# A two-layer cross-attention and feed-forward kernel in fp32: four places in its order are rearranged, and TensorE's buffers start on multiples of 256 bytes

## What is computed

```
x = x + mlstm(layernorm(x), ctx, ctx)      # 16 heads of 32, gates, decay matrix, head norm
x = x + moe(layernorm(x))                  # rms norm, router, best 2 of 8 experts (512->256->512), shared expert
x = x + attention(layernorm(x), ctx)       # q, k, v = 512 -> 2048, rms norm of q and k, 16 heads of 128,
                                           # two softmaxes: context tokens before 257 and from 257 on
x = x + last_ffn(layernorm(x))             # ternary weight (round(w/mean|w|), clipped) * mean|w|, plus bias
...
mlstm:  C = (q k^T / sqrt(32)) * D;  h = (C / max(|sum C|, exp(-max log D))) v;  head norm of h
moe:    sum over the two chosen experts of p_e * down_e(silu(gate_e(t)) * up_e(t)), plus the shared expert
q = rms_norm(x @ q_w + q_b);  k = rms_norm(ctx @ k_w + k_b);  v = ctx @ v_w + v_b;  out = softmax(q k^T / sqrt(128)) v @ o_w + o_b
```

## Time and profile before

| what | us |
|---|---|
| median of 3 runs (lowest, highest) | 1330.21 (1328.85, 1332.80) |
| the profiled execution, its own time | 1327.5 |
| its span, first to last instruction | 1325.8 |
| PE busy | 1272.9 (96%) |
| DVE busy | 840.4 (63%) |
| ACT busy | 739.3 (56%) |
| POOL busy | 391.7 (30%) |
| mean granted TensorE clock | 0.993 of full |

### The profile page before, as it was taken

How to read it: one execution, slowest core, us unless ns; L and a number is a source line. 1 busy time by engine, 2 the same in 40 slices (tenths; PEclk the granted TensorE clock), 3 DMA queues, 4 the chain that set the end, 5 groups by cost and what they waited for, 6 DMA issues and landing times. The chain is left out here.

```text
span 1325.8 us, 24459 instructions
## 1 busy us (share of the span) xinstructions
PE 1272.9 (96%) x7380; PEld 1056.3 (80%) x7381; DVE 840.4 (63%) x1611; ACT 739.3 (56%) x1829; POOL 391.7 (30%) x363
## 2 busy tenths in 40 slices
PE   7999997998999899999999999999999999999998
PEld 6787875776777778788877778878888888888987
DVE  3644647778679863544445577463587777777965
ACT  5225538788886441445555455554786556556551
POOL 0111015273728016599531332163010000000041
PEclk9999999999999899999999999999999999999999
DMA  7897399887865394665669776555375565555403
GB/s 251 306 365 257 133 319 347 264 274 249 280 213 183 68 359 171 221 189 174 205 206 317 238 267 191 180 192 192 119 231 162 157 165 158 158 170 153 120 26 127
DMA packets 165831, 277.06 MB, mean 209 GB/s; under 512 B 29744, under 2 KB 57136, under 8 KB 165488
## 3 DMA queue, kind: packets, MB, share of 16 engines
q1 hardware_dynamic: 139648, 219.46, 51.8%
q0 software_dynamic: 8960, 30.41, 7.0%
q10 hardware_dynamic: 17136, 26.09, 5.3%
HBM read 167.11 MB, written 108.80 MB: 208 GB/s over the span
## 5 line engine op out<-in xcount | busy, mean ns | idle before, releaser
L121 PE MATMUL banks<-of_shared_split,key_lead 128*128 128x512 f32 x256 | 104.6, 409 | 6.7 <-DVE key_trail L1427 6.3
L3019 ACT ACTIVATE prob<-banks,attend_row,rq 128x128 f32<-128x128 f32 x248 | 110.5, 470 | 0.0
L3032 ACT ACTIVATE attend_ol<-banks,of_attend_vbias 128x512 fp32r<-128x512 f32 x64 | 44.2, 691 | 116.5 <-PE banks L3231 116.5
L121 PE MATMUL banks<-wo,attend_ol 128*128 (+1 forms) x256 | 106.2, 415 | 0.0
L121 PE MATMUL banks<-queries_rows_split,queries_wl 128*128 128x512 f32 x256 | 100.9, 394 | 0.2 <-DVE queries_rows_split L2655 0.2
L123 PE MATMUL banks<-wo,attend_ot 128*128 (+1 forms) x256 | 100.7, 393 | 0.0
L123 PE MATMUL banks<-of_shared_split,key_trail 128*128 128x512 f32 x256 | 100.6, 393 | 0.0
L122 PE MATMUL banks<-of_shared_split,key_lead 128*128 128x512 f32 x256 | 100.1, 391 | 0.0
L122 PE MATMUL banks<-wo,attend_ol 128*128 (+1 forms) x256 | 99.9, 390 | 0.0
L123 PE MATMUL banks<-queries_rows_split,queries_wt 128*128 128x512 f32 x256 | 99.8, 390 | 0.0
L122 PE MATMUL banks<-queries_rows_split,queries_wl 128*128 128x512 f32 x256 | 99.8, 390 | 0.0
(11 more groups left out here) (407 smaller groups left out, 3507.3 us busy)
## 6 DMA issues: line engine op xcount, KB each, us to landing
mlstm_gmax<-running_max SPq DMA_DIRECT2D x32, 512.0 KB, 6.4
k_heads<-heads_key ACTq DMA_DIRECT2D x64, 256.0 KB, 4.9
q_heads<-queries_head SPq DMA_DIRECT2D x64, 256.0 KB, 2.8
q_ahead<-q_heads SPq DMA_DIRECT2D x64, 256.0 KB, 4.1
of_attend_k<-k_heads SPq DMA_DIRECT2D x60, 256.0 KB, 4.0
of_attend_v<-v_heads SPq DMA_DIRECT2D x60, 256.0 KB, 3.3
key_raw<-in_L_xattn_ki_w SPq DMA_DIRECT2D x20, 512.0 KB, 5.8
sorted_rows<-of_shared_split SPq DMA_DIRECT2D x2, 5120.0 KB, 27.3
```

The source lines that it names most:

```text
L121: nc.tensor.matmul(out, lead_l, lead_r, start=first, stop=False)
L3019: ins = nc.scalar.activation(prob[:, j % 2, b, :], ps[:, j % 2, b * S:(b + 1) * S], ACT.Exp, bias=row[:, j % 2, 1, b:b + 1], scale=rq[:, b ...
L3032: nc.scalar.activation(ol[:, par, j, :], ps[:, 4 + j % 2, :], ACT.Identity, bias=vbias[:, bass.ds(quad_of(it) * 4 + j, 1)]).then_inc(ol_do ...
```

## The change

It has seven parts.

1. Start: POOL's fills move from their own block into that of `values_and_gates`. SP loads the first context group in four pieces of 128 columns, each ahead of a weight load. PE begins with 10 idle transposes and turns 0 and 1; turn c+2 stands behind unit chunk c, and turns 4 to 7 behind chunk 2. ACT's `keep_even` stands one step later.
2. Values: DVE's trail cuts of weight quad 1 stand one unit later.
3. Heads, opening: a key unit more stands ahead of step 4's scores and the later ones move up; DVE does two `context_sum` before the first `decayed`, and decayed(2) and (3) earlier; SP issues `next_raw(0, 1)` before the body.
4. Heads, end: the 16 token sums stand behind the last four key units, three each, and the last four ahead of the third tail unit. DVE's `finish(PER)` stands ahead of the head scaling; ACT's `keep_tail(2)` stands behind the root.
5. Second pass: the down weights of experts 6 and 7 are cut by POOL after its first two parked loads, which no longer wait for tiles; ACT cuts and keeps tile 4 between the first copies of results.
6. Queries' end: 20 idle transposes for 14.
7. Places: padding tensors and new constants put of_shared_split, the context, keys, routed tiles, queries, `parked`, `wo` and the attention's tiles on multiples of 256 bytes.

```diff
-PARKED = 146144
+PARKED = 146432
 TAIL = (1, G - 1)
-TAIL_W, TAIL_V = 119328, 193568
-WO, Q_AHEAD = 129760, 195296
+TAIL_W, TAIL_V = 119552, 193792
+WO, Q_AHEAD = 130048, 195584
 PROB = Q_AHEAD + 4 * N * 4
-X_LEAD, X_TRAIL = 115232, 59712
-KEY_RAW, KEY_SPLIT = 160288, 195104
+X_LEAD, X_TRAIL = 115456, 59712
+KEY_RAW, KEY_SPLIT = 160512, 195328
...
-        TRAILS = {OPENS[q + 1] - (6 if q < QUADS - 2 else 5) + c: (q + 1, c) for q in range(QUADS - 1) for c in range(C)}
+        TRAILS = {OPENS[q + 1] - (6 if 0 < q < QUADS - 2 else 5) + c: (q + 1, c) for q in range(QUADS - 1) for c in range(C)}
...
-            load_ctx(0)
             for c in range(C):
+                sp.dma_start(stage[0][:, :, c * P:(c + 1) * P],
+                             a["ctx_2048"][0:GB, :, c * P:(c + 1) * P].rearrange("b s d -> s b d")).then_inc(ctx_first[c], 16)
                 sp.dma_start(raw[:, c, :], w_dram[c * P:(c + 1) * P, 0:N]).then_inc(first_loaded[c], 16)
...
+            setup(nc, K, pool, blank, made)
...
+            keep_even(0)
             turn_plain(C)
+            keep_even(2)
             turn_plain(C + 1)
-            keep_even(0)
-            keep_even(2)
...
-            for t in range(C):
-                turn(t)
+            pe.wait_ge(made, 1)
+            keep_busy(nc, ps[:, 0, :], K.ident, 10)
+            turn(0)
+            turn(1)
             for c in range(C):
                 first_chunk(c)
-                if c < C - 1:
-                    turn(C + c)
+                if c + 2 < C:
+                    turn(c + 2)
                 if c == C - 2:
-                    turn(C + c + 1)
+                    for t in range(C, 2 * C):
+                        turn(t)
...
-    OPENING = (0, 1, 2, 3, 5, 6, 8, 9, 11, 12, 14, 15)
+    OPENING = (-1, 0, 1, 2, 3, 5, 6, 8, 9, 11, 13, 15)
...
+            next_raw(0, 1)
...
-            for b in range(TAIL_IN_HEADS):
+            for b in range(TAIL_IN_HEADS - 1):
                 keep_tail(b)
             act.wait_ge(sums, 1)
             nc.scalar.activation(rk[:], ps[:, 2, 0:B], ACT.Sqrt, scale=1.0 / INNER, bias=K.eps6[:, 0:1]).then_inc(rk_done, 1)
             act.wait_ge(late_agg, 1)
             nc.scalar.activation(K.rstd[:, EARLY:], K.mv[:, EARLY:, 1], ACT.Sqrt, bias=K.eps5[:, 0:1]).then_inc(late_root, 1)
+            keep_tail(TAIL_IN_HEADS - 1)
...
-                    if n + 1 < PER or g + 1 < G:
+                    if (n + 1 < PER or g + 1 < G) and not (first and n < 3):
                         decayed(g, n + 1, first)
+                    if first and n == 0:
+                        decayed(g, 2, first)
                     if first:
                         keys_at(g, n, 1, weight_trail, first)
+                    if first and n == 1:
+                        decayed(g, 3, first)
...
-            for b in range(GB):
-                context_sum(0, b)
+            context_sum(0, 0)
+            context_sum(0, 1)
             decayed(0, 0, True)
+            context_sum(0, 2)
+            context_sum(0, 3)
+            decayed(0, 1, True)
...
+            finish(PER)
             dve.wait_ge(fac_done, G)
             for b in range(GB):
                 r = slice(b * H0, (b + 1) * H0)
                 ins = nc.vector.tensor_tensor(sq[:, r, :], raw_heads(last)[:, r, :],
                                               small[:, 5, r].unsqueeze(2).broadcast_to([P, H0, DH0]), ALU.mult)
             own(ins)
-            finish(PER)
...
+            def token_sums(tokens):
+                for b in tokens:
+                    ins = nc.tensor.matmul(ps[:, 2, b:b + 1], total[:, b * S:(b + 1) * S], K.ones[:, 0:1],
+                                           start=True, stop=True)
+                return ins
+
+            pe.wait_ge(total_done, CLOSES[G - 2] + 1)
+            pe.wait_ge(c_done, UNITS)
             for m in range(PER - LAG, PER):
                 keys(G - 1, m)
+                token_sums(range(3 * (m - PER + LAG), 3 * (m - PER + LAG) + 3))
             pe.wait_ge(tail_loaded, 32)
             pe.wait_ge(h_done, G * QUADS)
             tail_unit(nc, ps, split, tail_w, 0).then_inc(tail_product, 1)
             for b in range(1, TAIL_IN_HEADS):
                 if TAIL_BANKS[b] in KEY_BANKS:
                     pe.wait_ge(ksq_done, UNITS)
+                if b == TAIL_IN_HEADS - 1:
+                    pe.wait_ge(total_done, UNITS)
+                    token_sums(range((G - 1) * GB, B)).then_inc(sums, 1)
                 tail_unit(nc, ps, split, tail_w, b).then_inc(tail_product, 1)
-            pe.wait_ge(total_done, UNITS)
-            for b in range(B):
-                ins = nc.tensor.matmul(ps[:, 2, b:b + 1], total[:, b * S:(b + 1) * S], K.ones[:, 0:1],
-                                       start=True, stop=True)
-            ins.then_inc(sums, 1)
...
+    outer.sb("line", [P, 40])
...
+    inner.sb("line", [P, 16])
...
+            BY_POOL = (E - 2, E - 1)
...
-                pool.wait_ge(down, 1 + 5 * piece // 2)
+                if piece == 2:
+                    for e in BY_POOL:
+                        pool.wait_ge(dn_loaded[e % 4], 32)
+                        pool.wait_ge(dn_ready, e)
+                        n, ins = cut_by_pool(wd[:, e], raw_dn[e % 4], n)
+                        ins.then_inc(dn_ready, 1)
+                if piece >= 2:
+                    pool.wait_ge(down, 1 + 5 * piece // 2)
...
-            for e in range(4, E):
+            for e in range(4, E - 2):
                 act.wait_ge(dn_loaded[e % 4], 32)
                 nc.scalar.activation(wd[:, e, 0], raw_dn[e % 4], ACT.Copy).then_inc(dn_lead, 1)
-            for n in range(2):
+            keep((0, 0))
+            hidden_lead((0, H_DEEP))
+            for n in range(1, H_DEEP - 1):
                 keep((0, n))
-            second(act, second_slot, skip=H_DEEP)
+            second(act, second_slot, skip=H_DEEP + 1)
...
-            keep_busy(nc, ps[:, 7, :], K.ident, 14)
+            keep_busy(nc, ps[:, 7, :], K.ident, 20)
...
+    ph.sb("line", [P, 16])
...
+        kept("attend_line", [P, 56])
```

36 lines of the change are left out of this document (18 added, 18 removed).

## The result

The changed kernel took 1336.98 us (median of 11 runs, 1334.16 to 1340.91), the kernel before 1330.78 (11 runs, 1327.82 to 1336.16). The ratio is 1.0043, with a 95% interval of 1.0028 to 1.0059. I had forecast 1321 and a range up to 1332, so both the sign and the range were wrong. The profiled execution took 1339.07 us, its span is 1337.4.

What follows compares the result with a forecast made beforehand. PE was taken to bound the kernel, busy 1272.9 of 1325.8 us. The terms -2.0 - 2.3 - 2.0 + 0.6 + 2.3 - 0.8 - 4.5 sum to -8.7 us, so 1321 on the median, range 1303 to 1332.

Steps and rivals of the forecast that it cites:

- Heads, opening: Opening of the heads: an earlier key unit and DVE's earlier `cmat` shorten PE's waits; -2.0 us, bounds 0 and -4.2.
- the slower rival: All operands: equal offsets at 0 are the worst pair, +23 us on the pace, about 1349; chance 0.06.
- Second pass: Routed second pass: tile 4's wait goes, but tile 8 waits 5.0 us for POOL; +2.3 us, bounds -3.9 and +6.
- goes as meant: Second pass: tile 8 does not wait for POOL, so -3.9 replaces +2.3, 1315 us; chance 0.09.
- Places: Value, key, shared, x and tail products: multiples of 256 bytes bring 226.7 ns; -4.5 us, bounds 0 and -9.
- the floor at 226.7 ns: Matmul pace: 226.7 ns, the best that any window showed at any offset, taken as the floor.
- the fast one: All 4,250 matmuls: offsets between multiples cost part of 13.3 ns; 42 to 57 us won, about 1275; chance 0.10.
- the places are worth nothing: Matmul pace: it follows something other than offsets; -4.2 or less remains, 1326 to 1330; chance 0.22.
- Start and values: Kernel start, earlier first unit, -2.0 us (-3.3 to -1.0); values, PE's wait for turn 15's trail goes, -2.3.
- the weight's trail hides: Values: the fourth weight trail, one unit later, still has two units before its quad opens, so costs nothing.
- Heads, end: End of the heads: moved token sums worth 0, ACT's later third-tail-unit copy costs +0.6 us, bounds -1.0 and +1.5.
- queries' end: End of the queries: six more idle transposes may hold the clock, winning 1.5 to 1.7 us or 0; -0.8 taken.

Runs made afterwards that it cites:

- the earlier parts: The changed kernel with SP's eight loads of the next key group's context parts at steps 2 to 9 instead of 4 to 11: 0.9991, 1329.97 us.
- unchained: The changed kernel with context parts loaded earlier and POOL cutting experts 6 and 7 without waiting for DVE's order: 0.9985, 1325.62 us.

## Why the prediction was wrong

- **Heads, opening**: the step that failed. I took -2.0, bounds 0 and -4.2; it is +6 to +7. I said that the key units "are only moved" and looked at who waits for DVE. A unit that is moved forward also needs its own operands earlier, and the row on `ctx_split` (0.4 us of waiting before) said that they arrived just in time. I had no bound on the side of a loss, though the units were moved past SP's queue as well. With the load moved as well the opening is worth about 1 us, inside the scatter of the profiles, though its waits fell as forecast. Of the rivals none had this cause; the slower rival was about the places.
- **Second pass**: right in its mechanism; the stall of 5.0 us at tile 8 was 4.9, tile 4's wait went, and POOL's last trail ended at 706.0, 697.7 on the old scale where 697 was forecast. Forecast +2.3; taking it out gave 2.0 on the changed kernel and 4.3 with the earlier parts, and the profiled stage is 4.2 longer. The sign is safe, the size only within 2 to 4 us. The rival "goes as meant" is out. What I did not see is that even unchained it wins nothing that can be told from the scatter, since POOL slows DVE and tile 4 waits as long as before.
- **Places**: a term that was mis-sized, -4.5 for a measured -1.5 to -1.9. The mechanism holds where pace is even (x, tail, shared: 1.8 us, as predicted for them). The 3.1 us that the sum had for values and keys (1,392 matmuls at 2.2 to 2.3 ns) were not there: the mean of these stages did not move by more than 0.3 ns. Of the rivals, the floor at 226.7 ns stands, and so the fast one is out; "the places are worth nothing" is out by the paces, though the times alone would allow it. The Trainium skill's page SBUF — State Buffer, section Specifications, counts lines of 16 bytes. By that rule the x products could not have changed, and they did, by 6.4 ns.
- **Start and values**: forecast -4.3, measured -3.1. The first unit is 3.8 us earlier; eight transposes moved behind it take 0.9 of that back, and in some executions six matmuls or more at half pace another 1.2 or more. (The lower clock at the start, in the prediction as well, is read from this pace; the profile's column of the granted clock has 1.00 there.) The values' 2.3 depends on the execution: in the run on this part alone the stall is gone, in the changed kernel's profile 1.7 of it is back. I said that the weight's trail hides, and there it is what PE waits for at 60.8 us, behind DVE's own wait for x from DRAM. That I gave this term no bounds was wrong.
- **Heads, end** and **queries' end**: +0.6 and -0.8 forecast; together +0.7 measured, not clear of 0 and inside the bounds. The profiles have +0.4 to +1.7 for the first. For the second, the 20 transposes held the clock in 5 of 11 profiles.

Corrected by the measured parts, the sum is -3.1 (start and values) + 7 (opening) + 2.0 (second pass) - 1.5 (places) + 0.7 (heads' end and transposes) = +5.1 us, against 5.7 measured. Each term is known to some 2 or 3 us, so that they meet so closely is in part luck; only the opening's is larger than that.

## To carry to other kernels

When work on the bounding engine is moved forward, list what each moved unit reads and when that lands, above all loads whose wait is a few tenths today: they have no slack, and a step of 3 us turns into a wait of 8. Cutting work off a busy engine to an idle one is a gain only if the two don't slow each other and if nobody gates on the slower one. And take a pace from the mean of a whole stage, not from one clean stretch.

## What the runs showed of the hardware

- POOL and VectorE slow each other when both work on fp32 tiles in the buffers: a 128x1024 subtraction of DVE took 1.22 us alone, 1.64 beside POOL's one-input instruction, and 2.3 beside its two-input one (twice, in the kernels with POOL unchained); POOL's two-input instruction of 128x512 took 1.29 us alone and 2.25 there.
- In undisturbed stretches a 512-column matmul followed the last by 226.7 to 226.9 ns when both operands started at the same offset from a multiple of 256 bytes (0, 32 and 224 were seen), and by 233.3 with 32 for the moved and 96 for the stationary one. In values and keys 17 to 29% of the matmuls run at 232 to 236 ns whatever the places, and in the first routed pass, with equal offsets throughout, the mean goes from 228.9 ns (96) to 229.5 (0) and 231.0 (32); why is open.
- In eleven profiles PE was idle for 2.1 to 2.4 us at the joint of the routed passes. In seven of them the granted clock of the 3.4 us behind was 0.52 to 0.69, in four it stayed at 1.00, and two kernels with the same code there fell on either side. Behind the six idle times of 3.1 to 4.9 us it was 0.50 to 0.71 each time.
